# Mixer, recurrence and feed-forward in one program: another order between the first two, the last squares summed on TensorE, finished rows in another tile, weight sums at other tiles

## What is computed

```python
x = _layernorm(x + _L0_attn_ref(x, ...))   # Mamba-2 mixer: 16 heads of 64, state 16
x = _layernorm(x + _L0_ffn_ref(x, ...))    # x @ weight * scale, length bounded by tanh and 0.99
x = _layernorm(x + _L1_attn_ref(x, ...))   # gated linear recurrence, width 512
x = _layernorm(x + _L1_ffn_ref(x, ...))    # silu(x Wg) * (x Wu) @ Wd, integer weights, width 2048
```

## Time and profile before

| | us |
|---|---|
| median of 3 runs (lowest, highest) | 1044.23 (1041.99, 1044.94) |
| the profiled execution, its time | 1042.84 |
| the profiled execution, its span | 1041.1 |

### The profile page before, as it was taken

How to read it: one execution, slowest core, us unless ns; L and a number is a source line. 1 busy time by engine, 2 the same in 40 slices (tenths; PEclk the granted TensorE clock), 3 DMA queues, 4 the chain that set the end, 5 groups by cost and what they waited for, 6 DMA issues and landing times.

```text
span 1041.1 us, 19629 instructions
## 1 busy us (share of the span) xinstructions
PE 998.1 (96%) x7374; PEld 832.3 (80%) x7374; DVE 809.3 (78%) x1431; ACT 645.6 (62%) x1337; POOL 335.6 (32%) x462
## 2 busy tenths in 40 slices
PE   5899999999999997899999999999899999999997
PEld 5889898999989885799999999986445875875873
DVE  5998999899999998747766866885858766766763
ACT  6968786867777684564666566567232762762760
POOL 2004234152414135243435344333231331331331
PEclk9999999999999998999999999999999999999999
DMA  7530413213040346500011011223411201201001
GB/s 228 186 114 25 138 41 119 104 57 146 14 154 8 137 133 201 198 17 27 16 43 42 1 42 41 72 81 122 180 44 51 72 2 52 72 1 51 31 2 60
DMA packets 44702, 81.36 MB, mean 78 GB/s; under 512 B 7360, under 2 KB 17600, under 8 KB 42560
## 3 DMA queue, kind: packets, MB, share of 16 engines
q1 hardware_dynamic: 44608, 80.11, 22.5%
HBM read 67.24 MB, written 12.85 MB: 77 GB/s over the span
## 4 chain that ended last, share of the span: by engine, by line
PE 73%; DVE 12%; ACT 6%; POOL 3%; issue 3%; DMA 2%; SPq 1%; POOLq 0%; DVEq 0%; ACTq 0%
PE banks L820 24%; PE banks L2204 14%; PE banks L2272 11%; PE banks L1552 8%; PE banks L1520 4%; PE banks L2195 4%; PE banks L942 2%; PE banks L890 1%; PE banks L934 1%; PE banks L919 1%; DVE c_gx L1399 1%; DVE c_cv L1375 1%; DMA c_xb<-tokens 1%; DVE c_xb L1354 1%; PE banks L2175 1%
## 5 line engine op out<-in xcount | busy, mean ns | idle before, releaser
L2272 PE MATMUL banks<-d_wd,d_hh 128*128 128x512 f16 x256 | 97.0, 379 | 0.0
L2272 PE MATMUL banks<-d_wd,d_hl 128*128 128x512 f16 x256 | 97.0, 379 | 0.0
L654 DVE SCALAR_TENSOR_TENSOR a_xs<-a_xpre,a_cvec,a_xs 128x256 f32<-128x256 f32 x192 | 91.3, 543 | 0.1
L1848 POOL TENSOR_TENSOR d_hl<-d_h32s,d_hh 128x512 f16<-128x512 f32 x48 | 55.6, 1159 | 98.2 <-ACT d_hh L1943 98.2
L820 PE MATMUL banks<-a_xth,a_wxh 128*128 128x256 f32 x256 | 75.6, 296 | 3.3 <-ACT a_xs L455 3.3
L679 DVE TENSOR_TENSOR_SCAN a_L<-a_L,a_ident 128x512 f32<-128x512 f32 x64 | 74.8, 1212 | 0.5
L820 PE MATMUL banks<-a_xth,a_wgh 128*128 128x256 f32 x256 | 73.8, 288 | 0.5 <-ACT a_sg L484 0.5
L820 PE MATMUL banks<-a_xtl,a_wxh 128*128 128x256 f32 x256 | 73.3, 286 | 0.0
L820 PE MATMUL banks<-a_xth,a_wxl 128*128 128x256 f32 x256 | 73.2, 286 | 0.0
L820 PE MATMUL banks<-a_xth,a_wgl 128*128 128x256 f32 x256 | 71.8, 280 | 0.0
L820 PE MATMUL banks<-a_xtl,a_wgh 128*128 128x256 f32 x256 | 71.7, 280 | 0.0
(11 more groups left out here) (347 smaller groups left out, 3278.3 us busy)
## 6 DMA issues: line engine op xcount, KB each, us to landing
a_L<-decays SPq DMA_DIRECT2D x16, 1024.0 KB, 4.8
a_xf<-in_x_turned SPq DMA_DIRECT2D x16, 256.0 KB, 3.8
a_xr<-in_x SPq DMA_DIRECT2D x16, 256.0 KB, 2.9
tokens<-a_xr SPq DMA_DIRECT2D x16, 256.0 KB, 2.0
c_xb<-tokens SPq DMA_DIRECT2D x16, 256.0 KB, 3.0
...
```

The costliest lines, as they stand in the source:

```text
L654: ins = dve.scalar_tensor_tensor(out=out, in0=xpre[:, m, k:k + T], scalar=cvec[:, m, k:k + 1], in1=out, op0=ALU.mult, op1=ALU.add)
L1848: pool.tensor_tensor(hl[:, m, :], (h32s[:, m % 4, :] if i else h32[:, m % 2, :]), hh[:, m, :], ALU.subtract).then_inc(s_hl, 1)
L2272: ins = pe.matmul(ps_o[:, c % 2, :], h[:, m, cols(c)], wd[:, m, :], start=(m == 0 and h is hh), stop=(m == M - 1 and h is hl), skip_group_ ...
```

## The change

- Mixer to recurrence: on every engine, the calls at the end of the mixer and the start of the recurrence stand in another order. On SP the constants, the pieces of `y` and `ag` and the rows of step 1 are sent for before the store of step 6 and the residual rows of step 7 rather than after. On DVE the last step runs `gating(14)` ahead of `scaled(0)` and `low(14)` ahead of the rest. On PE `turn(0)` comes after the last `out_proj` and `sum_sq`, `turn_in(1)` comes between the halves of the `x` projection, and the wait for the last `residual` moves from the loop's head to the `y` projection. The last two `normalize` run on ACT in place of DVE. The pieces `NW + 5` are split later, `softplus(1)` too, and ACT waits for it only at `decay(0)`. On POOL `out_bias(0)` comes after `edges(0)`, which DVE's convolution waits for.
- TensorE sums its last squares: for chunks 14 and 15 `sum_sq` takes eight matmuls and POOL's two trees go.
- Recurrence: `norm(s)` writes the sum with the output projection into `finished(s)`, not into the slot, and `load_x(s + 3)`, which refills the slot, waits for that sum (`s_res`), not for the normalised rows (`s_ln`).
- FFN: the eight `weight_sums` stand at blocks 9, 11, 13, 15 and, two each, after the results of token blocks 1 and 2; before, at blocks 7, 8, 9, 10, 12, 14 and two after token block 1.

```diff
@@ -295,9 +295,9 @@
                     load_piece(NW + 1)
+                    sp.wait_ge(s_gate, 4 * NS)
+                    following_stage["constants"]()
+                    load_piece(NW + 2)
+                    load_piece(NW + 3)
+                    following_stage["load_x"](1)
                 store(s - 1)
         residual(NS - 1)
-        sp.wait_ge(s_gate, 4 * NS)
-        following_stage["constants"]()
-        load_piece(NW + 2)
-        load_piece(NW + 3)
-        following_stage["load_x"](1)
         sp.wait_ge(s_yp, R * C * NS)
@@ -381,8 +381,6 @@
         following_stage["bound"](0)
-        tree(C * NS - 2)
         following_stage["bounded_norm"](0)
-        tree(C * NS - 1)
         scale(C * NS - 2)
-        scale(C * NS - 1)
         norm(C * NS - 2)
+        scale(C * NS - 1)
         norm(C * NS - 1)
@@ -565,17 +563,18 @@
                 evict(s + 1, 1)
-            else:
-                following_stage["square"](0)
             high_y(C * s)
-        square(C * NS - 2)
+        following_stage["square"](0)
         following_stage["softplus"](0)
         following_stage["tanh"](0)
+        square(C * NS - 2)
         high_y(C * NS - 1)
         square(C * NS - 1)
+        following_stage["softplus"](1)
         high_piece(NW + 2)
-        following_stage["turn"](0)
-        following_stage["turn_in"](1)
         high_piece(NW + 3)
-        following_stage["softplus"](1)
+        following_stage["turn"](0)
+        normalize(C * NS - 2)
         high_piece(NW + 4)
-        high_piece(NW + 5)
+        following_stage["turn_in"](1)
+        normalize(C * NS - 1)
+        return {"high_piece": lambda: high_piece(NW + 5)}
@@ -635,8 +634,2 @@
-        def normalize(n):
-            j = n % C
-            out = xr[:, j, :]
-            dve.wait_ge(s_std, n + 1)
-            dve.tensor_scalar(out, out, mv[:, j, 0:1], mv[:, j, 2:3], ALU.subtract, ALU.mult).then_inc(s_done, 1)
-
         def conv_pair(s, p):
@@ -783,3 +776,11 @@
             if s + 1 == NS:
+                following_stage["softplus_in"]()
+                gating(C * s)
                 following_stage["scaled"](0)
+                low(C * s)
+                output(C * s + 1, 0)
+                output(C * s + 1, 1)
+                gating(C * s + 1)
+                update(C * s + 1)
+                break
             gating(C * s)
@@ -792,7 +793,6 @@
             low(C * s)
-            if s + 1 < NS:
-                steps_in(s + 1)
+            steps_in(s + 1)
             gating(C * s + 1)
-        following_stage["softplus"](0)
         low(C * NS - 1)
+        following_stage["softplus"](0)
         following_stage["bounded"](0)
@@ -801,13 +801,11 @@
         mean_sq(C * NS - 2)
-        following_stage["turn"](0)
         residual(C * NS - 2)
-        low_piece(NW + 2)
         mean_sq(C * NS - 1)
-        normalize(C * NS - 2)
+        following_stage["turn"](0)
         residual(C * NS - 1)
+        low_piece(NW + 2)
         following_stage["turn_in"](1)
-        normalize(C * NS - 1)
         low_piece(NW + 3)
-        following_stage["softplus"](1)
-        return {"low_piece": (lambda: low_piece(NW + 4), lambda: low_piece(NW + 5))}
+        low_piece(NW + 4)
+        return {"low_piece": lambda: low_piece(NW + 5)}
@@ -861,9 +859,10 @@
             j = n % C
-            if n == 0:
-                pe.wait_ge(s_sq, 1)
-            else:
+            whole = 0 < n < C * NS - C
+            if whole:
                 pe.wait_ge(s_tree, n)
+            else:
+                pe.wait_ge(s_sq, n + 1)
             wait(pe, s_rv, n)
             pe.wait_ge(s_ya, R * C * (n // C + 1))
-            parts = range(M if n == 0 else 1)
+            parts = range(1 if whole else M)
             for m in parts:
@@ -994,6 +993,5 @@
         out_proj(C * NS - 1, 0)
-        following_stage["turn"](0)
-        sum_sq(C * NS - 1)
         out_proj(C * NS - 1, 1)
-        following_stage["turn_in"](1)
+        sum_sq(C * NS - 1)
+        following_stage["turn"](0)
@@ -1107,3 +1105,3 @@
             for j in range(C):
-                wait(sp, s_ln, C * (s - SLOTS) + j + 1)
+                wait(sp, s_res, C * (s - SLOTS) + j + 1)
                 sp.dma_start(slot(s)[:, j, :], chunk(x_in, s, j)).then_inc(s_x[s % SLOTS][j], 16)
@@ -1195,7 +1193,8 @@
         def main(following_stage):
-            pool.wait_ge(s_bias, 16)
             pool.wait_ge(*last["output"])
-            out_bias(0)
             for s in range(NS):
                 edges(s)
+                if s == 0:
+                    pool.wait_ge(s_bias, 16)
+                    out_bias(0)
                 if s + 1 < NS:
@@ -1266,2 +1265,4 @@
             act.wait_ge(s_ga, M * s + M)
+            if s == 0:
+                act.wait_ge(s_sp, 3)
             for m in range(M):
@@ -1269,4 +1270,3 @@
-        def main(following_stage):
-            act.wait_ge(s_sp, 3)
+        def main(before, following_stage):
             for s in range(NS):
@@ -1286,2 +1286,4 @@
                     high_hy(s - 1)
+                else:
+                    before["high_piece"]()
                 if 0 < s < NS - 1:
@@ -1414,6 +1416,6 @@
             for j in range(C):
-                out = slot(s)[:, j, :]
+                out = finished(s)[:, j, :]
                 dve.wait_ge(s_out, C * s + j + 1)
                 dve.wait_ge(s_bo, C * s + j + 1)
-                dve.tensor_tensor(out, ps_o[:, j, :], out, ALU.add).then_inc(s_res, 1)
+                dve.tensor_tensor(out, ps_o[:, j, :], slot(s)[:, j, :], ALU.add).then_inc(s_res, 1)
                 dve.wait_ge(s_res, C * s + j + 1)
@@ -1425,5 +1427,5 @@
             for j in range(C):
-                out = slot(s)[:, j, :]
+                out = finished(s)[:, j, :]
                 dve.wait_ge(s_std, C * s + j + 1)
-                dve.tensor_scalar(finished(s)[:, j, :], out, mv[:, j, 0:1], mv[:, j, 2:3], ALU.subtract, ALU.mult).then_inc(s_ln, 1)
+                dve.tensor_scalar(out, out, mv[:, j, 0:1], mv[:, j, 2:3], ALU.subtract, ALU.mult).then_inc(s_ln, 1)
@@ -1432,6 +1434,8 @@
+        def softplus_in():
+            dve.wait_ge(s_small, 32)
+            dve.scalar_tensor_tensor(out=e, in0=z, scalar=-1.0, in1=z, op0=ALU.mult, op1=ALU.min).then_inc(s_sp, 1)
+
         def softplus(part):
             if part == 0:
-                dve.wait_ge(s_small, 32)
-                dve.scalar_tensor_tensor(out=e, in0=z, scalar=-1.0, in1=z, op0=ALU.mult, op1=ALU.min).then_inc(s_sp, 1)
                 dve.wait_ge(s_sp_act, 1)
@@ -1457,4 +1461,2 @@
                 if s == 0:
-                    for low_piece in before["low_piece"]:
-                        low_piece()
                     convolve(s)
@@ -1466,2 +1468,4 @@
                 low_conv(s)
+                if s == 0:
+                    softplus(1)
                 if s + 1 < NS:
@@ -1474,2 +1478,4 @@
                     turn(s + 1)
+                if s == 0:
+                    before["low_piece"]()
                 if s == NS - 2:
@@ -1565,4 +1571,2 @@
         def main(following_stage):
-            pe.wait_ge(*last["residual"])
-            pe.wait_ge(*last["mean_sq"])
             for s in range(NS):
@@ -1571,3 +1575,5 @@
                     pe.wait_ge(*split["x"])
-                project(ps_a, W["x"], xth, xtl, lambda q: wait(pe, s_ga, M * (s - 1) + 2 * q + 2), s_xb)
+                    pe.wait_ge(*last["mean_sq"])
+                project(ps_a, W["x"], xth, xtl, lambda q: wait(pe, s_ga, M * (s - 1) + 2 * q + 2), s_xb,
+                        between=None if s else lambda: turn_in(1))
                 if s + 1 < NS:
@@ -1576,2 +1582,3 @@
                     pe.wait_ge(*split["y"])
+                    pe.wait_ge(*last["residual"])
                 project(ps_b, W["y"], xth, xtl, lambda q: wait(pe, s_gx, M * (s - 1) + 2 * q + 2), s_yp)
@@ -2146,6 +2153,6 @@
                             convert(M + n)
-                    if 7 <= m < 10:
-                        weight_sums(0, 2 * m - 14)
-                    if m in (10, 12, 14):
-                        weight_sums(1, m - 10)
+                    if m in (9, 13):
+                        weight_sums(0, (m - 9) // 2)
+                    if m in (11, 15):
+                        weight_sums(1, (m - 11) // 2)
                     product(i, m)
@@ -2160,5 +2167,5 @@
                         blocks(i + 1)
-                    if i == 0 and c == 1:
-                        weight_sums(0, 6)
-                        weight_sums(1, 6)
+                    if i == 0 and 0 < c < 3:
+                        weight_sums(0, 2 * c + 2)
+                        weight_sums(1, 2 * c + 2)
@@ -2211,3 +2218,3 @@
             if n < NP and n % 2 == 0:
-                pe.wait_ge(s_sums, {0: 4, 2: 5, 4: 6, 6: 8}[n])
+                pe.wait_ge(s_sums, n + 2)
             s_half_h.wait(pe, HALF_H.get((21, n - 2), 0))
```

24 lines of the change are left out of this document (12 added, 12 removed).

## The result

| | before | changed |
|---|---|---|
| median of the runs | 1044.36 us (4 runs) | 1036.26 us (4 runs, 1035.77 to 1037.3) |
| the profiled execution, and its span | 1042.84, 1041.1 | 1036.09, 1034.4 |
| ratio | | 0.993, 95% interval 0.9914 to 0.9946 |

Faster by 8.1 us in the medians and by 6.7 in the two profiled executions. The forecast was 12.3 against the profiled execution and 13.2 against the median. So the sign held, the time lies inside the range (0.7 from its slow end), and the sum did not hold: some 5 us are missing.

A forecast was written before the change was run, and what follows sets the result against it. TensorE, busy 96% of the span, was taken to bound the kernel. The terms 7.9 + 3.4 + 3.1 - 2.1 = 12.3 us gave 1030.5 from the profiled execution and 1031.9 from the median; forecast 1031, range 1025.5 to 1037.

The forecast's parts named there:

- Transition, 7.9: Mixer to recurrence, up to the end of `turn(1)`: PE gets there at 446.8 instead of 454.74, gain 7.9 us.
- the collision of `out_bias` with `convolve`: Recurrence step 0: POOL's bias add now runs beside DVE's convolution, which takes 1.7 us more.
- the low clock in the `x` projection: Transition: one stretch of PE at the lower clock was allowed for, costing 1.9 us.
- the waits before `ag` and at `turn(1)`: Transition: new PE waits of 0.5 us before `ag` and 1.6 for the second half at `turn(1)`.
- Recurrence, 3.4: Recurrence's `turn_in`: all five waits for landing rows should go, gaining 3.4 of 3.6 us, bounds 0 and 3.6.
- FFN gate stage, 3.1: FFN `gate_up`: moved weight sums shrink PE's wait of 2.0 to 0.4, two others go; gain 3.1 us.
- Second tile, -2.1: FFN's second tile: two more sums between results 2 and 3 lose 2.1 us, bounds 0.5 and 4.5.
- The first of the recurrence's: Rival: the recurrence's wait only changes its name, `c_cvh` replacing the DMA wait; 1034.4 us, chance 0.12.
- That the FFN gives back more than it gets: Rival in the FFN: the late `result(3)` costs 4.5 us, not 2.1; 1033.4 us, chance 0.10.
- Neither collision nor low clock: Rival in the transition: neither comes, 3.6 us better, 1027 us; chance 0.15.
- The slower case: Rival: the lower clock stays from the sums of squares through `x`, `bounded(1)`, `y`; 1050 us, chance 0.03.

The follow-up runs named there:

- the trees: The changed kernel with POOL's trees folding the last two sums of squares again, one column each on TensorE: 1039.8 us, ratio 0.9961 to the kernel before.

## Why the prediction was right and wrong

- **Transition, 7.9: right in its mechanism,** by its own steps, and a little high: 8.0 in the lead, of which 0.6 came earlier, and 6.8 between the means of several profiles. `low(14)`'s end, the sums of squares (1.84 for a whole one), `x` at 414.82, the collision of `out_bias` with `convolve` (forecast 1.7 more, measured 7.10 - 5.11 = 2.0) and `turn(1)` at 446.75 all came as priced. Two errors nearly cancelled, which was luck: the low clock in the `x` projection (window rows above) cost 2.4 (9.0 to `bounded(1)` against 6.6 at full clock) where 1.9 was allowed for, and the waits before `ag` and at `turn(1)` were 0.3 and 0.9, not 0.5 and 1.6.
- **Recurrence, 3.4: this is the step that failed.** "So the chain through ACT and DVE is as long as PE's own work, and PE just fits": from that equality the prediction took nearly the whole wait as gain. From the start of the second sigmoid of `ig` (ACT, 485.71 in the change) to the end of `c_cvh` (507.79 + 1.06) the chain takes 23.1; PE takes `c_cvh` at 508.90, 0.05 later, so it now runs at the chain's pace. Half a microsecond of four of the waits had run beside this chain, and 2.1 of the 3.6 were gained up to step 7. The second fault is larger: I followed the gain for one step only. Carried to the last step, PE meets `c_hyl` there, which was late even before (0.7), and waits 2.9; with the stretch of lower clock behind it, that took all the 2.1 back. With this part alone the ratio gives 0.1 us, not 3.4.
- **FFN gate stage, 3.1: the size was off,** 1.7 in the trace. The wait of 2.0 shrank to 0.43, as forecast, and the two of 0.76 went. But "Blocks 9, 11, 13 and 15 have 2 to 3 us to spare" was read from DVE's distance to PE, and left out DVE's own DMA: 1.35 of wait came at block 11. Bounds 2 and 3.6 did not hold it.
- **Second tile, -2.1: right** (1.7 in waits, -2.0 in the lead). The two FFN terms together are nothing, which the kernel with this part alone confirms.
- **Rivals.** The first of the recurrence's, given 0.12, came in part: `c_cvh` did take the place of the DMA waits, for some half a microsecond each, but most of the 3.4 went at `c_hyl` in the last step, which no rival named, and its time of 1034.4 was passed by 1.9. No rival named the DMA in front of `product(11)`. That the FFN gives back more than it gets (0.10) came true by the gain and not, as it said, by the loss. Neither collision nor low clock: both came. The slower case did not.

What stays open: why the stretch of lower clock behind the `c_hyl` wait comes in one profile of the change and not in the next, what the trees cost beyond step 1, and what would remove the 1.57 in front of the `x` projection.
